# Moving operand splits, router gating and h2 steps between the block products of a four-layer LoRA kernel

## The reference

```python
x = x + _L0_cond_ref(x, L0_cond_weight, L0_cond_scale_log, condB_codebook, L0_cond_lora_A, L0_cond_lora_B)
x = x + _L1_cond_ref(x, itok_B_0_7, L1_cond_W, L1_cond_Wr, L1_cond_A, L1_cond_B)
x = x + _L2_cond_ref(x, itok_B_0_23, L2_cond_W, L2_cond_b, L2_cond_lora_As, L2_cond_lora_Bs)
x = x + _L3_cond_ref(x, itok_B_0_15, L3_cond_weight)
# layer 0: weight plus LoRA delta, quantized to a codebook in groups of 128, then x @ w_eff.T
# layer 1: a linear layer plus 8 LoRA experts of rank 16, the best two by a router
logits = jnp.einsum('btd,ed->bte', x, Wr) + bias[:, None, :]
topw, topi = jax.lax.top_k(logits, TOP_K)
weights = jax.nn.softmax(topw, axis=-1)
gates = jnp.sum(jax.nn.one_hot(topi, E) * weights[..., None], axis=-2)
h = jnp.einsum('btd,erd->bter', x, A)
out = base + SCALING * jnp.einsum('bter,bte,eor->bto', h, gates, B)
# layer 2: a linear layer with bias, plus a LoRA adapter of rank 16 chosen for each batch
# layer 3: one of 16 whole weights for each batch
return jnp.einsum('bsi,boi->bso', x, weight[adapter_ids])
```

## Time and profile before

| | us |
|---|---|
| median of 3 runs | 658.16 (657.95 to 658.24) |
| the profiled execution | 658.05 |
| its span, first to last instruction | 656.2 |
| PE busy in the span | 644.5 |
| DVE busy | 499.8 |
| ACT busy | 364.1 |
| POOL busy | 89.0 |

### The profile page before, as it was taken

One profiled execution on the slowest core, in us unless ns is written; L12 is line 12 of the kernel. 1 busy time (PEld: TensorE's weight loads), 2 busy tenths in 40 slices (PEclk: granted clock), 3 DMA queues, 4 the chain that ended last, 5 costly groups with the idle time before them and its releaser, 6 DMA issues.

```text
span 656.2 us, 10322 instructions
## 1 busy us (share of the span) xinstructions
PE 644.5 (98%) x3992; PEld 591.0 (90%) x3992; DVE 499.8 (76%) x645; ACT 364.1 (55%) x549; POOL 89.0 (14%) x120
## 2 busy tenths in 40 slices
PE   8999999999999999899999999999999999999997
PEld 8899989999999999898889899889989889989886
DVE  6899899879970649858876967887886888686753
ACT  6673674961911445637664735664745665564553
POOL 2210225005010010001130001221001122000010
PEclk9999999999999999999999999999999999999999
DMA  9663112121021002132773122673213575002472
GB/s 295 190 200 91 33 35 62 33 62 35 1 64 64 1 1 89 33 97 72 231 237 98 52 75 61 197 255 124 65 33 97 162 258 182 1 1 65 127 229 94
DMA packets 46020, 67.32 MB, mean 103 GB/s; under 512 B 3604, under 2 KB 32020, under 8 KB 45972
## 3 DMA queue, kind: packets, MB, share of 16 engines
q1 hardware_dynamic: 40900, 58.28, 28.6%
q10 hardware_dynamic: 5072, 8.39, 3.5%
HBM read 58.27 MB, written 8.39 MB: 102 GB/s over the span
## 4 chain that ended last, share of the span: by engine, by line
PE 85%; DVE 13%; issue 1%; ACT 1%; DMA 1%; DVEq 0%; ACTq 0%
PE ps L1260 26%; PE ps L1262 26%; PE ps L1261 26%; DVE e_both L897 4%; PE ps L1403 3%; DVE x_both L897 2%; DVE tmp L1187 1%; PE ps L1271 1%; PE ps L1432 1%; PE ps L1405 1%; DMA xraw<-lora_b_t 1%; ACT e_both L683 1%; DVE bc_hi L897 1%; DVE e_mid_w L1160 0%; DVE e_mid_w L1123 0%
## 5 line engine op out<-in xcount | busy, mean ns | idle before, releaser
L1260 PE MATMUL ps<-e_both,ring_hi 128*128 128x384 f32 (+3 forms) x384 | 133.6, 348 | 0.0
L1262 PE MATMUL ps<-e_both,ring_lo 128*128 128x384 f32 (+3 forms) x384 | 133.5, 348 | 0.0
L1261 PE MATMUL ps<-x_both,e_both 128*128 128x256 f32 x448 | 125.6, 280 | 0.0
L897 DVE TENSOR_TENSOR e_both<-raw,e_both 128x512 fp32r<-128x512 f32 x128 | 90.3, 725 | 34.1 <-ACT e_both L771 33.4
L771 ACT ACTIVATE e_both<-raw 128x512 fp32r<-128x512 f32 x128 | 78.9, 628 | 67.0 <-PE ps L1262 66.7
L1260 PE MATMUL ps<-e_both,e_mid 128*128 128x512 f32 (+2 forms) x288 | 110.8, 385 | 0.0
L1262 PE MATMUL ps<-e_both,e_mid 128*128 128x512 f32 (+2 forms) x288 | 110.7, 384 | 0.0
L1261 PE MATMUL ps<-e_both,e_mid 128*128 128x512 f32 (+2 forms) x288 | 110.6, 384 | 0.0
L587 POOL TENSOR_TENSOR raw<-raw,ident 128x128 f32<-128x128 f32 x64 | 42.3, 662 | 360.7 <-DMA raw<-w_t 360.7
L1261 PEld LDWEIGHTS ps<-x_both,e_both 128*128 128x128 f32 x448 | 84.6, 189 | 0.0
L1262 PEld LDWEIGHTS ps<-e_both,ring_lo 128*128 128x128 f32 x384 | 72.3, 188 | 5.7
(11 more groups left out here) (175 smaller groups left out, 1271.0 us busy)
## 6 DMA issues: line engine op xcount, KB each, us to landing
raw<-w_t SPq DMA_DIRECT2D x64, 512.0 KB, 4.4
w_w<-x_t SPq DMA_DIRECT2D x16, 512.0 KB, 3.9
w_w<-w SPq DMA_DIRECT2D x15, 512.0 KB, 4.2
y<-tmp ACTq DMA_DIRECT2D x30, 256.0 KB, 3.5
e_both_w<-w_t SPq DMA_DIRECT2D x5, 512.0 KB, 7.7
e_both_w<-w_t SPq DMA_DIRECT2D x4, 384.0 KB, 6.0
e_mid_w<-bs SPq DMA_DIRECT2D x24, 64.0 KB, 2.9
e_mid_w<-b_cat SPq DMA_DIRECT2D x4, 128.0 KB, 5.9
```

The costliest lines, as they stand in the source:

```text
L897: return dve.tensor_tensor(out, whole, hi.bitcast(F32), ALU.subtract)
L1260: pe.matmul(out, a[0], b_[0], start=start, stop=False, **kw)
L1261: pe.matmul(out, a[0], b_[1], start=False, stop=False, **kw)
L1262: return pe.matmul(out, a[1], b_[0], start=False, stop=stop, **kw)
```

## The change

Nothing is added or removed; instructions change places in the lists of three engines.

- ACT: the copies for h2 and the Exp move from around S4 to behind the second keep of bank 0; A22 moves ahead of the copies of the turned gates and of h2.
- DVE: T3 moves ahead of S2; S4 moves out of the gating to ahead of it, and S3 takes its place between the two parts of the gating; A12 follows the gating, ahead of the adapter halves and T4; the block sum of bank 0, with its wait for the fifth product, moves ahead of the low half of the turned gates; A22 moves ahead of the h2 additions.
- PE: the transposes move from behind the fourth product to behind the fifth, `h2_add` from behind the fifth to behind the sixth.

```diff
--- before.py
+++ after.py
@@ -813,28 +813,28 @@
                 act.wait_ge(s_bs, 96 * (g + 1))
                 for h in range(2):
                     act.activation(bs_half[h], bs_raw[:, h * 512:(h + 1) * 512], ACT.Copy).then_inc(bs_hi1, 1)
-                act.wait_ge(tok_done, g + 1)
-                act.wait_ge(h2_clear, 1)
-                for j in range(2):
-                    act.activation(h2_tok[:, 2 * j:2 * j + 2, R2 * j:R2 * (j + 1)],
-                                   tok[:, 2 * j:2 * j + 2, NOW_AT[j]:NOW_AT[j] + R2], ACT.Copy).then_inc(h2_tok_done, 1)
                 split_weight(g, "S4")
-                act.wait_ge(gate, GATE_STEPS * g + GATE_DV)
-                act.activation(gw[:, 1, :], gw[:, 0, :], ACT.Exp).then_inc(e_exp, 1)
                 act.wait_ge(prod, NP * g + 2)
                 keep(2, x3_sum[1][1], 4)
                 split_x(g, "T4")
                 split_weight(g, "S3")
                 act.wait_ge(prod, NP * g + 3)
                 keep(0, x3_sum[0][1], 0)
+                act.wait_ge(tok_done, g + 1)
+                act.wait_ge(h2_clear, 1)
+                for j in range(2):
+                    act.activation(h2_tok[:, 2 * j:2 * j + 2, R2 * j:R2 * (j + 1)],
+                                   tok[:, 2 * j:2 * j + 2, NOW_AT[j]:NOW_AT[j] + R2], ACT.Copy).then_inc(h2_tok_done, 1)
+                act.wait_ge(gate, GATE_STEPS * g + GATE_DV)
+                act.activation(gw[:, 1, :], gw[:, 0, :], ACT.Exp).then_inc(e_exp, 1)
                 split_weight(g, "A12")
+                split_weight(g, "A22")
                 act.wait_ge(gt_mm, g + 1)
                 act.activation(gt_hi, ps[:, 7, :], ACT.Copy).then_inc(gt_hi_done, 1)
 
                 for t in range(4):
                     act.activation(h2_sum[:, t * P:(t + 1) * P], ps[32 * t:32 * (t + 1), 6, 0:P], ACT.Copy, scale=2.0
                                    ).then_inc(h2_turned, 1)
-                split_weight(g, "A22")
                 act.wait_ge(h2_summed, 2 * (g + 1))
                 for i in range(2):
                     act.activation(h2_k[32 * i:32 * (i + 1), :], h2_sum, ACT.Copy).then_inc(h2_hi_done, 1)
@@ -1144,7 +1144,7 @@
                 step(dve.tensor_tensor(gw[:, 0, :], mx[:, 1, :], mx[:, 0, :], ALU.subtract))
                 assert n[0] == GATE_DV
 
-                split_weight(g, "S4")
+                split_weight(g, "S3")
                 dve.wait_ge(e_exp, g + 1)
                 step(dve.tensor_scalar(gw[:, 2, :], gw[:, 1, :], 1.0, None, ALU.add))
                 step(dve.reciprocal(gw[:, 3, :], gw[:, 2, :]))
@@ -1180,33 +1180,32 @@
                 dve.wait_ge(e_add, 4 * g + 2)
                 split_weight(g, "S1")
                 dve.tensor_tensor(s4_whole, weight[0][1], s2_whole, ALU.subtract).then_inc(e_add, 1)
+                split_x(g, "T3")
                 split_weight(g, "S2")
                 if g:
                     for i in range(4):
                         dve.wait_ge(y_out[i], 16 * 2 * g)
                 dve.tensor_tensor(s3_whole, weight[0][0], weight[1][0], ALU.subtract).then_inc(e_add, 1)
+                split_weight(g, "S4")
                 gating(g)
-                split_x(g, "T3")
+                split_weight(g, "A12")
                 for h in range(2):
                     dve.wait_ge(bs_hi1, 2 * g + h + 1)
                     v = bs_half[h][32:64, :]
                     minus(v, bs_raw[32:64, h * 512:(h + 1) * 512], v).then_inc(bs_done, 1)
                 split_x(g, "T4")
-                split_weight(g, "S3")
-                split_weight(g, "A12")
+                dve.wait_ge(prod, NP * g + 5)
+                dve.wait_ge(c_copy, 4 * g + 2)
+                sum_block(0, x3_sum[1][1], x3_sum[1][1])
                 dve.wait_ge(gt_hi_done, g + 1)
                 minus(gt_lo, ps[:, 7, :], gt_hi).then_inc(gt_done, 1)
+                split_weight(g, "A22")
                 dve.wait_ge(h2t_mm, g + 1)
                 dve.wait_ge(h2_turned, 4 * (g + 1))
                 for i in range(2):
                     dve.scalar_tensor_tensor(out=h2_sum, in0=ps[32 * i:32 * (i + 1), 6, :], scalar=2.0, in1=h2_sum,
                                              op0=ALU.mult, op1=ALU.add).then_inc(h2_summed, 1)
                     dve.wait_ge(h2_summed, 2 * g + i + 1)
-
-                dve.wait_ge(prod, NP * g + 5)
-                dve.wait_ge(c_copy, 4 * g + 2)
-                sum_block(0, x3_sum[1][1], x3_sum[1][1])
-                split_weight(g, "A22")
                 dve.wait_ge(h2_hi_done, 2 * (g + 1))
                 minus(h2_k[64:96, :], h2_sum, h2_k[0:32, :]).then_inc(h2_done, 1)
                 split_w3(g, 0, 0)
@@ -1516,12 +1515,12 @@
                 block_product(g, 2, False)
                 pe.wait_ge(c_copy, 4 * g + 2)
                 block_product(g, 3, False)
+                pe.wait_ge(c_copy, 4 * g + 3)
+                block_product(g, 4, False)
                 turn_h2(g)
                 turn_g(g)
-                pe.wait_ge(c_copy, 4 * g + 3)
-                block_product(g, 4, False)
+                block_product(g, 5, True)
                 h2_add(g)
-                block_product(g, 5, True)
                 pe.wait_ge(c_sum, 4 * g + 1)
                 block_product(g, 6, False)
                 pe.wait_ge(h2_done, g + 1)
```

## The result

The changed kernel takes 649.78 us (median; 649.50 to 650.14), the kernel before 658.06 beside it (657.94 to 658.24): a ratio of 0.9874, interval 0.9857 to 0.9891. A second set of runs gave 649.85 (649.57 to 650.30) against 657.78, ratio 0.9879 (0.9864 to 0.9894). The profiled execution took 649.50, its span is 647.7. I had predicted 650.4 with a range from 649.9 to 652.4.

The account below looks back on a forecast made before the run. TensorE, busy 98% of the span, bounds the kernel. Four groups at 163.04 instead of 170.76 us remove 7.72 of stall and restart: 658.05 - 7.72 = 650.33, with 0.11 for the runs' median 650.4, range 649.9 to 652.4.

Parts of the forecast that it names:

- The bound and the place: TensorE busy 98%, so only its idle time, about 12 us, can be won; four waits, 5.8 us, before each group's fifth product.
- The schedule: New order placed on the second group's clock, products starting at 351.72 and gates at 392.48, each operand ready before its product.
- Sum done: DVE's block sum of bank 0, behind the fifth product's end: done at 382, before the last product at 386.80.
- Tail: L1202 twice, two ACT copies and one low half behind the h2 addition: about 3.8 us, ending 390.8, before gates at 392.48.
- The cover of S3: Fifth product: DVE's first low half of S3 ready at 371.9, needed at 374.44, so 2.5 us early.
- S2's cover of 1.45: First group: S2's first low half, pushed by T3, done at 258.3 for a product at 259.75; smallest slack of all.
- The sum: Whole kernel: 658.05 minus 7.72 us of stall and restart in four groups gives 650.33 for the profiled execution.
- the time of an unstalled group: First product to gates without waits: seven products of 5.68, transposes 0.55, h2 addition 0.45, 40.76 us.
- The range: Whole kernel: 0.5 us down for restart; up to 652.4 for the tail's 0.6 bound and part of possible operand misses.
- The first: DVE's wait for the fifth product holds gates and A22; PE waits 2.05 us per group, 658.6, no change; chance 0.06.
- The second: An operand narrowly misses its product in every group, 0.6 to 1 us each, 652.8 to 654.4; chance 0.08.
- The third, the reloads: Fifth tile's reload at the y product, 3.8 us later, delays PE in each group: 665.6, slower; chance 0.03.

## Why the prediction came out as it did

**The bound and the place.** Right. But for the start of the kernel, told below, all of the gain lies between first product and gates, by the removal of the waits of the earlier trace rows, and at no clock below 1.00.

**The schedule.** The second group's products now begin 2.82 us sooner than on the clock that I had used, so my times less 2.82 can be held against the rows above. S4's high halves: 360.5 expected, 360.52 measured. S3's first low half done: 369.1, 367.79 + 1.22 = 369.01. Sum done: 379.2, 378.96. Tail begun and ended: 384.2 and 388.0, 384.13 and 387.64. Gates: 389.66, 389.59. The cover of S3 is 371.60 - 369.01 = 2.6 (I wrote 2.5), that of the tail 1.95 (1.7), and both were tried by delays. In the first group, S2's cover of 1.45 held; no product waits there.

**The sum.** Too small, 7.72 for 8.00. The step that failed is the time of an unstalled group, 7 x 5.68 + 0.55 + 0.45 = 40.76. I read one product's pace and used it for seven. The rows of the changed kernel show 5.68 for A11 (348.90 to 354.58), 5.69 for S4 (365.91 to 371.60), but 5.65 for S3 (371.60 to 377.25) and for the last (383.94 to 389.59). S2, by its start at 360.26, takes 5.65 as well. Transposes with the product behind them take 383.47 - 377.25 = 6.22 where I had 6.23, but that is luck: the transposes are 0.46 (377.25 to 377.71), not 0.55, and the product 5.76, not 5.68. Three times 0.03, less 0.02 for the h2 addition (383.47 to 383.94 is 0.47), is the 0.07 per group, 0.28 in all. The last product's 5.66 could have been read in the trace of before, from its first row, below, to the gates at 394.30:

```profile
388.64 0.28 PE L1260 MATMUL ps<-ring_hi,e_both 128*128 128x256 f32 x1
```

**The range.** Its lower end left 0.5 us below 650.4, and the median came out 0.62 below: 0.28 went with the sum, and 0.34 is left. For the profiled execution the cause of its rest is seen: it began its token phase 0.52 us sooner than that of before, in a phase that the change does not touch. Two profiles of the same kernel differ there by 0.46, so this is scatter. For the medians scatter is likely and not shown, as the other executions have no profile. I had started from 658.16, the median of three runs of before within 0.3 us, and taken that spread for the kernel's own; the three later sets of before have medians of 657.78, 657.90 and 657.94, with single runs from 657.51 to 658.41. With either miss alone the range would have held: 650.4 - 0.28 is 650.1. The wide side, 2 us upward for operands that miss, was not needed.

**ACT's moves.** Under-told. I had priced the move of the Exp and S4 by the small wait that it removes, 0.4 us in the first group. The run with T3 alone shows their larger part: they pay for T3's place in the first group, where PE would otherwise wait 1.5 us for the keep behind the Exp. I had asked only whether S2 could bear the delay, and not what stands behind S2 on DVE and waits on ACT.

**PE's moves.** I gave them no price of their own. With the moves on ACT and DVE that they allow they are worth 0.83 us beside operands that already come first, and alone they cost 28 us.

**The rivals.** The first, that the wait for the fifth product makes the two queues serial, failed: ACT's A22 (377.45) and DVE's sum (377.74) ran side by side, and DVE idled for 1.02 us behind the sum. What a fixed queue can cost is seen in the run with PE's order of before, where the h2 copies behind A22 on ACT held PE 3.7 us. The second failed as well, no operand misses. The third, the reloads, failed with its number: the fifth tile was ready on POOL and split by ACT so:

```profile
392.39 0.46 POOL L587 TENSOR_TENSOR raw<-raw,ident 128x128 f32<-128x128 f32 x1 [48.52 <-DMA raw<-w_t]
```

```profile
404.52 0.63 ACT L771 ACTIVATE e_both<-raw 128x512 fp32r<-128x512 f32 x1 [0.83 <-PE ps L1261]
```

That is a lead of 404.52 - 392.85 = 11.7 us instead of 13.3. A further delay of 3.4, in the run with the delayed tail, cost the y products nothing.

## What to carry to other kernels

When the bound engine waits at one place for one operand, list what stands ahead of that operand in the queue of the engine that makes it, and move out what nobody needs sooner; here two moves on VectorE removed that wait from all four groups. For each move, follow every instruction that it pushes to the engine behind it and to the group with the least idle time: a hole in most groups may be missing in the first, and then another list must change too. A sum that multiplies one pace by 28 wants that pace from more than one product, and a range wants the scatter of the start.

## What the hardware showed that I had not expected

A wait of PE can cost more than its length. Behind waits of 3.7 to 4.5 us (twelve of them in three kernels) the granted clock stood at half its level, 1.2 instead of 2.4 GHz, for a part of the next product, which took 6.6 to 8.5 us instead of 5.7. Behind waits of 1.5 us and less (the kernel before among them) it never fell. Behind four waits of 2.0 us, in the kernel with PE's moves alone, it fell once, in the first group (0.76, 7.26 us), where a wait of 0.36 had gone ahead of it one product earlier, and stayed at 1.00 three times (5.75 us); whether that earlier wait is the reason, no run shows. That the clock falls when TensorE idles is what the Trainium skill states in "TensorE: Matmul & The Clock Gate", Part 1; the trace agrees, and adds the price here: 8.5 us for four waits of 4.2 to 4.5. I had left the clock out of the expectations for the two halves of the change, and they came out 7 and 10 us slower than expected, mostly for it.
